# Norm sums, router weights and ratio pieces moved, and an exponential as a power on GpSimd, in a nine-stage language-model tower

## The reference

```
h = token_convolution(x)                    # 9 neighbouring ids, embedding rows, a 576 x 64 product
h = h + linear_attention(norm(h))           # elu + 1 features, 8 heads
h = h + routed_ffn(norm(h))                 # relu, 2 layers of a shared and a routed 128 x 128 expert
h = h + bn_attention(norm(h))               # softmax attention, batch norm over all tokens, relu, + x
h = h + moe(norm(h), 64->128->64, top 2)    # gelu experts weighted by a softmax of the top 2 of 8
h = h + window_attention(norm(h))           # 4 heads, window 16, rms norms, rotary, two gated groups
h = h + moe(norm(h), 64->64->64, top 2)     # tokens + gelu experts weighted by the top 2 of 8
h = h + rational_convolution(norm(h))       # FFT filter; response = numerator / denominator
h = h + depth_ffn(norm(h))                  # x + a gelu FFN on the 511 highest-weighted tokens of 1024
norm(x) = (x - mean(x)) / sqrt(var(x) + 1e-5)
```

## Time and profile before

| | |
|---|---|
| median of 3 runs | 755.84 us (753.54 to 755.95) |
| the profiled execution | 755.32 us |
| its span, first to last instruction | 753.5 us |
| mean granted TensorE clock | 0.894 |
| busy: TensorE, VectorE, ScalarE, GpSimd | 607.5, 487.1, 316.4, 241.9 us |
| stage starts | 0, 81.1, 135.6, 173.7, 264.2, 378.8, 519.4, 607.7, 708.0 us |

### The profile page before, as it was taken

One profiled execution on the slowest core, in us unless ns is written; L12 is line 12 of the kernel. 1 busy time (PEld: TensorE's weight loads), 2 busy tenths in 40 slices (PEclk: granted clock), 3 DMA queues, 4 the chain that ended last, 5 costly groups with the idle time before them and its releaser, 6 DMA issues. The chain is left out here.

```text
span 753.5 us, 13090 instructions
## 1 busy us (share of the span) xinstructions
PE 607.5 (81%) x4750; PEld 400.9 (53%) x4750; DVE 487.1 (65%) x1350; ACT 316.4 (42%) x667; POOL 241.9 (32%) x217
## 2 busy tenths in 40 slices
PE   3479476877886888998988999998778786998876
PEld 3267365665564452322286887786332132987543
DVE  1025567583755679689746888567856896744865
ACT  1023133544555653554415465421343246743254
POOL 6720596031300101001045867433300139600420
PEclk9779789888998669989999999788888999899989
DMA  6835730202000020000010000003100010000002
GB/s 203 284 93 147 213 93 1 74 3 60 1 1 1 0 76 0 1 0 1 1 39 14 7 14 9 13 2 88 52 1 0 1 38 0 3 3 2 0 3 55
DMA packets 18944, 30.06 MB, mean 40 GB/s; under 512 B 6466, under 2 KB 15810, under 8 KB 18242
## 3 DMA queue, kind: packets, MB, share of 16 engines
q1 hardware_dynamic: 16322, 19.81, 9.2%
q0 software_dynamic: 2560, 9.44, 4.1%
HBM read 27.26 MB, written 1.05 MB: 38 GB/s over the span
## 5 line engine op out<-in xcount | busy, mean ns | idle before, releaser
L177 POOL TENSOR_TENSOR norm_rstd<-norm_var,minus_half 128x16 f32<-128x16 f32 x16 | 47.0, 2941 | 294.3 <-DVE norm_var L171 294.3
L1371 ACT ACTIVATE m_g<-PS,w_slot 128x512 f32<-128x512 f32 x96 | 60.8, 684 | 72.1 <-PE PS L1424 72.0
L1313 DVE TENSOR_TENSOR m_gw<-m_g,PS 128x512 f32<-128x512 f32 x96 | 60.9, 676 | 17.4 <-ACT m_g L1371 8.5
L1424 PE MATMUL PS<-m_xT,w_slot 64*128 64x512 f32 x192 | 64.5, 662 | 4.3 <-ACT m_g L1371 4.2
L1448 PE MATMUL PS<-m_gw,w_slot 128*64 128x512 f32 x192 | 56.9, 663 | 1.2 <-DVE m_gw L1313 1.2
L106 PE MATMUL PS<-w_base 128*128 128x128 f32 x322 | 48.0, 301 | 1.4 <-DVE win_obias L1649 1.4
L106 PEld LDWEIGHTS PS<-w_base 128*128 128x128 f32 x322 | 41.0, 156 | 8.5 <-issue 6.0
L345 DVE COPY tok_windowsT<-PS 128x512 f32<-128x512 f32 x16 | 11.1, 691 | 44.9 <-remote 22.8
L284 PE MATMUL PS<-w_base,tok_windows 128*128 128x128 f32 x128 | 21.1, 328 | 23.4 <-DMA tok_windows<-in_emb,tok_ids 16.2
L1432 PE MATMUL PS<-m_gT,m_sel 48*128 48x512 bf16 x96 | 23.2, 400 | 18.6 <-DVE m_gw L1313 14.7
L147 DVE BATCH_NORM_STATS2 norm_halves<-H 128x6 f32<-128x64 f32 x256 | 34.2, 209 | 2.3 <-PEq L2847 2.1
(11 more groups left out here) (339 smaller groups left out, 1527.5 us busy)
## 6 DMA issues: line engine op xcount, KB each, us to landing
rff_routed<-in_routed SPq DMA_DIRECT2D x64, 129.0 KB, 2.5
w_slot<-in_w_rat SPq DMA_DIRECT2D x1, 1525.0 KB, 11.9
w_slot<-in_w_win SPq DMA_DIRECT2D x1, 1378.5 KB, 5.7
w_slot<-in_w_m SPq DMA_DIRECT2D x1, 1329.0 KB, 5.7
w_slot<-in_w_early SPq DMA_DIRECT2D x1, 1100.0 KB
rat_inv<-in_rat_taps SPq DMA_DIRECT2D x1, 1024.0 KB, 7.4
rat_hf<-in_rat_taps SPq DMA_DIRECT2D x1, 1024.0 KB, 7.9
out<-H SPq DMA_DIRECT2D x8, 128.0 KB, 2.2
```

What stands on the lines that cost most here:

```text
L177: nc.gpsimd.tensor_tensor(N.rstd[:], N.var[:], C.minus_half[:], ALU.pow).then_inc(S["norm_rstd"], 1)
L1313: nc.vector.tensor_tensor(gw[:, i % 2, half, :], g[:, i % 2, half, :], gate_bank[half], ALU.mult)\
L1371: nc.scalar.activation(g[:, i % 2, half, :], hid_bank[(n - 1) % 3], ACT.Gelu, bias=b1[:, s:s + 1])\
L1424: nc.tensor.matmul(hid_bank[n % 3], w1[lane(half), s, :], pair_of(xT, pair)[lane(half)], start=True, stop=True).then_inc(S["hid_ps"], 1)
```

## The change

It moves and converts, and computes the same values:
1. first stage: a tile euler, all e, set on GpSimd;
2. routed_ffn: normalise(1) is split; statistics and centring ahead of add_biases(0, 0), scaling between the two;
3. batch-norm attention, loop: statistics of the second half in the staircase's prologue (lag 2), centring at n = 3, scaling at n = 4;
4. its tail: denominators(1) and (2) behind the first sum, (3) ahead of the last turn, (4) and (5) after it; ScalarE moves SQUARED_FIRST pieces ahead of y; 4 rouse matmuls for 16;
5. both expert stages: exponentials leaves ScalarE's list and becomes a power on GpSimd, euler to the m2; in the second, the next stage's norm comes in four pieces over successive steps, and one scale moves from step 13 to 10;
6. windowed attention: rouse and the wait for H from n = 520, not 560;
7. rational convolution: the last ratio on VectorE, and TensorE waits per group, not for all;
8. depth routing: take_weights(w + 1) ahead of rank_tokens(w).

```diff
+            nc.gpsimd.memset(C.euler[:], 2.718281828459045)
...
+            norm_stats(nc, v, S, hx(1), N, 1)
+            norm_centre(nc, v, S, hx(1), N, xc)
             add_biases(0, 0)
+            norm_scale(nc, v, S, N, xc, xn, 1)
             add_biases(0, 1)
-            normalise(1)
...
+            def upper_stats(it, w):
+                if isinstance(it, int) and it == 0 and w == 0:
+                    norm_stats(nc, vec, S, hx(1), N, 1)
-                      (6, channel_sums)]
+                      (6, channel_sums), (2, upper_stats)]
...
+                if ahead and n == 3:
+                    norm_centre(nc, vec, S, hx(it + 1), N, xc)
                 if ahead and n == 4:
-                    norm_stats(nc, vec, S, hx(it + 1), N, it + 1)
-                if ahead and n == 5:
                     vec.wait_ge(S["h_plus_x"], it * W + W)
-                    norm_apply(nc, vec, S, hx(it + 1), N, xc, xn, it + 1)
+                    norm_scale(nc, vec, S, N, xc, xn, it + 1)
...
-            for s in range(2):
+            for s in range(SQUARED_FIRST):
                 C.denominators.move(act, s, [PS[2 + s % 2][:]])
...
             denominators(0)
-            denominators(1)
             pe.wait_ge(S["lower_sum"], CHUNKS + 1)
...
+            denominators(1)
+            denominators(2)
             pe.wait_ge(S["sum2"], 1)
...
-            denominators(2)
-            denominators(3)
             for c in range(CHUNKS):
+                if c == CHUNKS - 1:
+                    denominators(SQUARED_FIRST)
...
-            rouse(nc, C, PS[0][:, 0, :], 16)
+            rouse(nc, C, PS[0][:, 0, :], 4)
...
+            def exponentials(it):
+                pool.wait_ge(S["gate"], it * GATE_STEPS + 8)
+                nc.gpsimd.tensor_tensor(t.e[:], C.euler[:], t.m2[:], ALU.pow).then_inc(S["exp"], 1)
...
                 if not again:
                     add_x(it)
+                exponentials(it)
...
+            def prepare_piece(k):
...
+                if k == 0:
+                    v.wait_ge(S["h_new"], 2)
+                if k < 2:
+                    norm_halves(nc, M.S, x, M, 2 * k)
+                    norm_halves(nc, M.S, x, M, 2 * k + 1)
+                if k == 1:
+                    norm_sums(nc, v, M.S, M, 0)
+                if k == 2:
+                    norm_centre(nc, v, M.S, x, M, M.xc)
+                if k == 3:
+                    norm_scale(nc, v, M.S, M, M.xc, M.xn, 0)
...
-                nc.scalar.activation(t.e[:], t.m2[:], ACT.Exp).then_inc(S["exp"], 1)
-            exponentials(0)
-                    if plan.gate[1] == i:
-                        exponentials(1)
...
-                if n == 560:
+                if n == 520:
                     pe.wait_ge(S["h_new"], W + 1)
-                    if 560 <= n < 660:
+                    if 520 <= n < 660:
                         rouse(nc, C, PS[0][:, 1, :], 2 if n < 620 else 4)
...
-M2_SCALES = (4, 8, 9, 12, 13, 14, 15)
+M2_SCALES = (4, 8, 9, 10, 12, 14, 15)
...
-            for s in range(STEPS):
+            for s in range(STEPS - 1):
                 ratio(s)
...
+            v.wait_ge(S["terms"], STEPS)
+            nc.vector.tensor_tensor(to[:, 0], last[:, 0, 0], last[:, 1, 1], ALU.add).then_inc(S["ht_last"], 1)
+            nc.vector.tensor_tensor(to[:, 1], last[:, 0, 1], last[:, 1, 0], ALU.subtract).then_inc(S["ht_last"], 1)
...
-            pe.wait_ge(S["ht"], 2 * STEPS)
             for g in range(PAIRS // 2):
+                if g < 2:
+                    pe.wait_ge(S["terms"], STEPS - 1 + g)
+                if g < PAIRS // 2 - 2:
+                    pe.wait_ge(S["ht"], 2 * (g // 2) + 2)
+                else:
+                    pe.wait_ge(S["ht_last"], 2)
...
+                take_weights(it, 0)
                 for w in range(W):
+                    if w + 1 < W:
+                        take_weights(it, w + 1)
                     if it == 0 and w == 2:
                         normalise(1)
                     rank_tokens(it, w)
```

More of the change, by code:

```diff
@@ L985, in _ @@
                 nc.scalar.activation(junk[:, at], FT[:, at], ACT.Relu, bias=C["bna_beta"], scale=gain[:]).then_inc(S["y"], 1)
-            for s in range(2, SQUARED_TAIL):
+            for s in range(SQUARED_FIRST, SQUARED_TAIL):
                 C.denominators.move(act, s, [PS[2 + s % 2][:]])
@@ L1275, in ahead @@
                         expand(it, k)
+            def prepare_piece(k):
+                M, x = C.next_norm, lambda w: groups(chunk_of(H, 0, w))
+                M.prepared = True
+                if k == 0:
[9 more added lines that the diff above has]
+                    norm_scale(nc, v, M.S, M, M.xc, M.xn, 0)
             def add_output(pair):
@@ L1324, in _ @@
                     ahead(1, i)
-                elif i == n_round + plan.stats + SL // 2:
+                elif again and i == n_round + plan.stats + SL // 2:
                     v.wait_ge(S["h_new"], 2)
                     prepare_next(nc, v, H, C, True, False)
-                elif i == n_round + plan.apply + SL // 2:
+                elif again and i == n_round + plan.apply + SL // 2:
                     prepare_next(nc, v, H, C, False, True)
+                elif not again and i >= n_round + SL // 2:
+                    prepare_piece(i - n_round - SL // 2)
             if not again:
@@ L1347, in copy_x @@
                 ins.then_inc(S["xT"], 1)
-            def exponentials(it):
-                act.wait_ge(S["gate"], it * GATE_STEPS + 8)
-                nc.scalar.activation(t.e[:], t.m2[:], ACT.Exp).then_inc(S["exp"], 1)
             def copy_output(pair):
@@ L2060, in rational_convolution @@
         S = semaphores(nc, "rat",
-                        "zeros coef_ps terms ht xf_ps xf nyq nyq_done hf_ps bias hf_re hf_im ends prod_ps prod_even "
+                        "zeros coef_ps terms ht ht_last xf_ps xf nyq nyq_done hf_ps bias hf_re hf_im ends prod_ps prod_even "
                         "prod_odd prodT_ps x1 Y out_ps h_new")
@@ L2158, in _ @@
                     at_nyquist()
+            last, to = terms[:, (STEPS - 1) % 2], C.denominators.of(STEPS - 1)
+            v.wait_ge(S["terms"], STEPS)
+            nc.vector.tensor_tensor(to[:, 0], last[:, 0, 0], last[:, 1, 1], ALU.add).then_inc(S["ht_last"], 1)
+            nc.vector.tensor_tensor(to[:, 1], last[:, 0, 1], last[:, 1, 0], ALU.subtract).then_inc(S["ht_last"], 1)
             bend = C["rat_bend"]
+            v.wait_ge(S["ht"], 2 * STEPS - 2)
+            v.wait_ge(S["ht_last"], 2)
             v.wait_ge(S["nyq_done"], 1)
@@ L2229, in _ @@
                 ins.then_inc(S["xf"], 1)
-            act.wait_ge(S["ht"], 2 * STEPS)
+            act.wait_ge(S["ht"], 2 * STEPS - 2)
+            act.wait_ge(S["ht_last"], 2)
             for g in range(PAIRS // 2):
@@ L2815, in tower @@
         C.minus_half = minus_half
+        euler = ctx.enter_context(nc.sbuf_tensor("euler", [P, W * G4], F32))
+        C.euler = euler
         C.out = out
```

9 lines of the change are left out of this document (5 added, 4 removed).

## The result

The changed kernel takes 723.12 us (median of 4 runs, 720.86 to 726.05) against 755.83 us for the kernel before: ratio 0.9576, 95% interval 0.9527 to 0.9625. The forecast was 730, its range 723 to 741. So 32.7 us went where 26.3 were worked out. The four runs form two pairs, near 720.9 and near 725.7; the profiled execution is of the second pair, 725.36 us with a span of 723.3, which is 30.2 shorter than the span before.

What follows compares the result with a forecast made beforehand. TensorE was taken as the bound, so time could come only from its idle gaps and halved clock. Eight stage terms sum to 26.3 us: 755.3 less 26.3 is 729.0, 729.5 at the median, called 730; range 723 to 741.

Steps and rivals of the forecast that it cites:

- Routed stage: Routed feed-forward: TensorE's gap before the second half's norm goes, 3.8, plus 1.5 of clock: 5.3 us (3.5 to 6).
- The loop: Batch-norm attention loop: TensorE's 2.06 us idle goes, less 0.6 handed down the staircase and some waiting: 0.9 (-0.6 to 1.6).
- The tail: Batch-norm attention's end: y 1.9 us earlier, last move about 2.4 earlier, next opening perhaps slower: 3.0 (1.5 to 4.3).
- First experts: First expert stage: mid-stage gelu goes early without the exponential ahead, VectorE then carries the stretch: 1.0 us (0 to 2).
- Fillers: Windowed attention: twenty more filler transposes may bring the clock back early: 1.3 us gained (-2.5 to 3).
- Second experts: Second expert stage: start loses 1.7, middle gains 4.7 less 1 for clock, norm pieces gain 2.5: 4.5 us (2 to 6).
- Rational stage: Rational convolution: TensorE turns group by group from 634.1, readers' last group starts about 5.3 us earlier: 5.3 (3 to 6).
- Depth routing: Last stage: early weight copies remove TensorE's 4.36 us gap; ranks' scales bound the last turn near 727: 5.0 (3.5 to 5.7).
- A: Rival, expert stages: a power with varying exponent is dear; at 11.6 us each the time is 762; chance 0.04.
- B: Rival, expert stages: GpSimd's power blocks VectorE, up to 2.94 us at each of four places, so 741; chance 0.05.
- C: Rival, clock: every gap closed leaves another; parts 2, 7, 8 gain no clock, 4 and 6 lose: 739; chance 0.18.
- D: Rival: VectorE bounds routed, second expert and depth stages sooner; a third of those gains goes: 735; chance 0.20.

Runs made afterwards that it cites:

- part 2 alone: Kernel before, with only the routed stage's second-half statistics and centring put ahead of the bias adds and scaling between them: 732.81 us against 740.82, ratio 0.9874.
- the experiment: Changed kernel with batch-norm loop norm placement, second expert stage's norm pieces and last ratio's move to VectorE undone: 727.50 us, 3.0 more than the changed kernel.

## Why the prediction came out as it did

The direction and the places were right, and so was the kind of gain in all parts but the fifth and the last ratio of the eighth. The sum was 6.4 us short of the medians' difference and 3.9 short of the profiles'. That 723.12 lies inside the range is in part luck: its lower end is 723, and two of the four runs are below it. Most of what was missed is half clock that a removed gap took with it. The lengths below are each of one or two traces. By part:

1. **Nothing**, as said. The first two stages came out 1.1 us longer; no part is in them but the memset, and linear attention takes 54.3 to 57.5 us with the same code, so it is likely their scatter.
2. **Routed stage: right** (5.3 said, 5.7 measured). Missed was that it hands on: 1.1 us of the next loop belong to it.
3. **The loop: mis-sized.** Said 0.9, measured 3.5 between the profiles: 1.1 by part 2 alone, and 2.2 when it is undone. With the old routed stage before it the new loop takes 63.7 against 64.0, a gain of 0.3; with the new one 60.6 against 62.8. The 0.6 "handed down the staircase" was 0.1 (the fourth turn of the probabilities comes 5.76 us behind the third, the others 5.66; before 6.32). Not counted were two short stretches of half clock, 27.5 to 31.0 and 41.2 to 44.6 us into the stage: the new loop alone removes neither, part 2 alone the second, both together both. In six other runs of the changed loop one such stretch lies in it all the same, 10.7 or 37.3 us in, so where they fall is not set by these edits alone.
4. **The tail: right in kind, a little high**: y comes 1.6 earlier (said 1.9), ScalarE's last move is the new end and comes 1.4 earlier (said 2.4), together 2.6 for 3.0. The next opening is slower as said (gate logits at 6.44 us, not 5.90), which does not show in the first read of e (12.18 us in, 12.17 before). But the shorter filler is not the cause: with sixteen they come at 6.44 too.
5. **First experts: the term of 1.0 was zero.** The gelu did go early (53.4 us into the stage, not 56.3), but VectorE reads e at 58.45 us into the stage in both kernels, at 322.82 before and 312.16 after. Its own list, not ScalarE's, was the chain, as the row with no idle time before it already says.
6. **Fillers: the upper end.** No row decided between -2.5 and 3, and the middle was taken; measured 3.1, undone 3.0 lost. The half clock lasted 3.4 us instead of 13.7, and 13.6 again with the filler undone.
7. **Second experts: two terms mis-sized**, 2.2 us for 4.5. The middle gave 4.9 (said 4.7, less 1 for the clock). The start cost 1.9 by the read of e (said 1.7), but the second gate then started 4.0 later than with both exponentials on ScalarE, and 2.2 to 4.1 later than in the three runs with only the first one there; the prediction put this at nothing. The extra goes with more half clock ahead of the second gate, and differs from run to run. The pieces gave 1.5 (said 2.5).
8. **Rational stage: right, 1.5 short.** The first group was said to start at 637.9, 30.0 us into the stage, and starts at 30.0. But the readers then run at 1.00 us a group (ScalarE's at 622.03, 623.06 and 624.06) until they have caught up with TensorE, not at 1.33 from the start. The last ratio's move was counted as part of it; it is worth nothing by the rows of the experiment, and the wait per group 5.1 of the 6.8.
9. **Depth routing: mis-sized, as far off as the loop**, 7.6 for 5.0. The forecast let the ranks' scales bound the last turn near 727. They come at that time (702.06, 16.6 us into the stage, for 724.7 in old time), but TensorE waits for none of them: the last turn starts at 701.70 and the second pass at 701.97, without idle time between, since each of the four turned tiles has its own place in PSUM. And the rows behind the 4.36 us gap were at half clock before: two groups of hidden rows at 2.08 for 1.14 and the products behind them at 3.04 for 2.00, 2.9 us in all, of which the forecast counted nothing.

By the prediction's own signs of being wrong, the first and the second expert stage (0.0 of 1.0, 2.2 of 4.5) gained less than half their term; in the first VectorE had indeed no gap at that place. The signs of being right came: of three table loads in each expert stage one is left, the powers take 2.9 to 3.0 us, and the counterpart of 485 to 495 is at full clock.

The rivals: A (a dear power) is refuted by 2.9 to 3.0 us with the exponent varying. (In its price the 3.8 us from the gate's end to the second read is no row of before, where that read came 7.9 behind.) B is refuted: VectorE's rows beside the powers are as long as ever. The Trainium skill, "SBUF — State Buffer", section "SBUF: two separate sides", has a two-input VectorE operation fully blocked by a GpSimd one that reads SBUF; here the power does not do that (0.29 us for 128 columns beside 2.9 us of it), while GpSimd's adds slow such rows (0.48 to 0.93), a slowing and not a full block. C was half right with the wrong sign: the clock did decide much of what the parts are worth, but removing gaps gave more than was counted (parts 3, 6, 9) more often than less (7). D did not happen in the routed and the depth stage, and VectorE was the bound in part 5, which D did not name; how much of the second expert stage's shortfall is VectorE's is not shown.

## What to carry to other kernels

TensorE's idle time can cost more behind it, also in the next stage: in depth routing about 4 us of it came with 2.9 us of half-clock rows. Price a removed gap as the gap plus the half-clock rows after it, and a new gap likewise, and expect such a price to be off by a few microseconds, as the stretches fall elsewhere from one kernel to the next. Filler matmuls are to be tried and not counted on: they were worth 3 us in the windowed stage and nothing in the batch-norm tail. An instruction that waits in an engine's list blocks what stands behind it (copies behind a ranking, gelus behind an exponential): put those that release another engine first. Move an operation to an idle engine only where its reader is not already waiting: the same 3.0 us power gained 4.9 us in one place and lost 1.9 or more in another, and splitting the two gave the kernel with the best median.

## What was not expected of the hardware

- The half-clock stretches can repeat: two executions of the changed kernel on chips of one kind had eight of nine stages equal to 0.6 us and seven to 0.1 us, while in other runs the same stage code differed by up to 3 us (rational stage 93.5 to 96.6, second expert 83.0 to 86.1, batch-norm 83.9 to 85.8, and 87.6 behind the old routed stage).
- The first stage alone differs between chips by 14 us (66.2 to 67.5 against 80.5 to 81.7); no other stage differs like that between them.
- A power of 128 x 16 elements takes 2.9 to 3.0 us on GpSimd with a varying exponent as with a constant one.
